# A gated delta-rule layer on one core: half the heads of the recurrence run one block and a boundary behind the other half, without constant products

## The reference

```
q, k, v = silu(conv(x Wq)), silu(conv(x Wk)) * 128**-0.5, silu(conv(x Wv))
a = sigmoid(x Wa + ba); beta = sigmoid(x Wb + bb)
for each token t, for each batch and head:       # state St is 128 x 128
    err = St k_t - v_t
    St  = a_t[:, None] * St - (beta_t * err)[:, None] * k_t[None, :]
    o_t = St q_t
o = layernorm(o) * sigmoid(x Wg) @ Wo;  x = layernorm(x + o)
x = layernorm(x + (silu(x Wu') * (x Wg')) @ Wd')     # ternary weights
```

## Time and profile before

| | us |
|---|---|
| median of 3 runs | 3010.08 (3008.52 to 3022.21) |
| the profiled execution, its own time | 3009.76 |
| its span, first to last instruction | 3008.0 |
| recurrence, first transposes of chunk 0 to those of chunk 15 | 1193.5 |
| the last chunk | 63.0 |

### The profile page before, as it was taken

One profiled execution on the slowest core, in us unless ns is written; L12 is line 12 of the kernel. 1 busy time (PEld: TensorE's weight loads), 2 busy tenths in 40 slices (PEclk: granted clock), 3 DMA queues, 4 the chain that ended last, 5 costly groups with the idle time before them and its releaser, 6 DMA issues. The chain is left out here.

```text
span 3008.0 us, 57441 instructions
## 1 busy us (share of the span) xinstructions
PE 2714.6 (90%) x18366; PEld 2291.7 (76%) x18366; DVE 2046.7 (68%) x5887; ACT 1191.7 (40%) x2377; POOL 1441.0 (48%) x1214
## 2 busy tenths in 40 slices
PE   8999999999995888988898988989865898699999
PEld 6888888888885777777787777877754777588887
DVE  5767868767783777777767777677746887533333
ACT  4454454454542222222222222222257876433333
POOL 3545345355365877677767777677622231000000
PEclk9999999999997999899989999899967999899999
DMA  5564664665557544344434444444455552400000
GB/s 123 143 198 134 164 178 136 171 177 141 172 149 250 199 184 184 138 172 175 160 137 184 183 184 178 159 183 183 172 214 196 208 191 106 168 8 10 14 10 14
DMA packets 417363, 454.86 MB, mean 151 GB/s; under 512 B 122496, under 2 KB 367232, under 8 KB 393856
## 3 DMA queue, kind: packets, MB, share of 16 engines
q1 hardware_dynamic: 417152, 452.22, 44.8%
HBM read 321.49 MB, written 131.14 MB: 150 GB/s over the span
## 5 line engine op out<-in xcount | busy, mean ns | idle before, releaser
L355 PE MATMUL pa_ps<-pa_x_hi,pa_w_hi 128*128 128x512 f32 x1296 | 507.5, 392 | 9.6 <-ACT pa_y L298 5.4
L355 PE MATMUL pa_ps<-pa_x_lo,pa_w_hi 128*128 128x512 f32 x1296 | 504.9, 390 | 0.0
L355 PE MATMUL pa_ps<-pa_x_hi,pa_w_lo 128*128 128x512 f32 x1296 | 504.9, 390 | 0.0
L438 DVE SCALAR_TENSOR_TENSOR pa_cv<-pa_y,pa_taps,pa_cv 128x2048 f32<-128x2048 f32 x144 | 355.9, 2472 | 17.8
L748 POOL TENSOR_TENSOR pb_gb<-pb_gb,pb_ng 128x448 f32<-128x448 f32 (+6 forms) x448 | 330.8, 783 | 57.8 <-DMA pb_ng<-scratch_ng 55.9
L1069 DVE TENSOR_TENSOR pb_tmp<-pb_gb,pb_ps 128x112 f32<-128x112 f32 (+6 forms) x1792 | 328.2, 220 | 19.4 <-POOL pb_gb L748 8.1
L1074 DVE TENSOR_TENSOR pb_ps<-pb_ps,pb_tmp 128x112 f32<-128x112 f32 (+6 forms) x1792 | 331.3, 226 | 6.3 <-DVE pb_tmp L1069 3.2
L943 PEld LDWEIGHTS pb_ps<-pb_Gm,pb_XT 128*128 128x128 f32 x2048 | 253.0, 199 | 68.9 <-issue 39.2
L355 PEld LDWEIGHTS pa_ps<-pa_x_hi,pa_w_hi 128*128 128x128 f32 x1296 | 243.6, 188 | 68.0 <-ACT pa_y L298 10.3
L732 POOL TENSOR_TENSOR pb_UT<-pb_UT,pb_crow 128x1024 f32<-128x1024 f32 x120 | 281.8, 2359 | 21.0 <-DMA pb_crow<-scratch_crow 20.3
L355 PEld LDWEIGHTS pa_ps<-pa_x_hi,pa_w_lo 128*128 128x128 f32 x1296 | 243.6, 188 | 51.2
(11 more groups left out here) (191 smaller groups left out, 5453.1 us busy)
## 6 DMA issues: line engine op xcount, KB each, us to landing
pb_crow<-scratch_crow SPq DMA_DIRECT2D x30, 2048.0 KB, 9.6
pb_gb<-scratch_pairs SPq DMA_DIRECT2D x64, 896.0 KB, 8.4
pa_o_ng<-scratch_beta SPq DMA_DIRECT2D x16, 1024.0 KB, 7.9
scratch_ng<-pa_o_ng SPq DMA_DIRECT2D x16, 1024.0 KB, 4.5
...
```

Source lines behind the costliest of these rows:

```text
L355: last = nc.tensor.matmul(out, w[:, mat, k, :], xx[:, k, b * S:(b + 1) * S], start=(k == 0 and n == 0), stop=(k == KT - 1 and n == 2))
L438: nc.vector.scalar_tensor_tensor(out=out, in0=yy[:, :, k:k + S], scalar=tap(k), in1=out, op0=ALU.mult, op1=ALU.add).then_inc(s_tap, 1)
```

## The change

In the recurrence the chunk becomes a cycle. Half 1 now runs one block and a chunk's boundary behind half 0: a cycle takes half 0 through blocks 0 to 3 of chunk c and half 1 from block 3 of chunk c-1 (with its state updates 2 and 3 and its starts of chunk c) to block 2 of chunk c. There is a first cycle, 14 middle ones and a last one, and behind it half 1's last block alone. Each engine's list and SP's is written out anew in this order, the ring places are new numbers, `T_PAST`/`D_PAST` step over places that a first or last cycle leaves out, and many semaphores are split by half. FILL is all zero and every other `busy` call of the cycles is gone, so no constant product is issued. `key_products` becomes `key_product`, one of the two tiles at a time. A new buffer `ngx` holds half 1's gates of blocks 2 and 3 (one ACT copy a cycle), so that `ng` can be reloaded before half 1 has done. The gates of block 0 are multiplied in on POOL at the end of the cycle before. Work per chunk is otherwise the same.

In the core of the diff below the lines that are left out are mostly removed ones.

```diff
...
+        ngx = m.sb("ngx", [P, HALF, CH // 2])
...
-        T_XT, T_XT_LAST = [0, 5, 10, 14, 18, 22, 28, 30], [0, 4, 8, 10, 12, 14, 16, 18]
-        t_xt = lambda n, hf, more: (T_XT if more else T_XT_LAST)[2 * n + hf]
-        t_later = lambda hf, more: 2 + (5 if more else 4) * hf
-        t_first = lambda hf: 16 + 8 * hf
-
-
-        D_START, D_CH = 10, 32
-        d_cross = lambda n, hf, more: 26 + hf if n == NBL - 1 and more else 2 * n + hf
-        D_STATE = [6, 10, 16, 22]
-        D_S = [14, 15, 20, 21, 28, 29, 30, 31]
-        D_S_FIRST = [22, 23, 24, 25, 28, 29, 30, 31]
-
-        FILL = [0, 0, 0, 0, 2, 0, 2, 4]
+        T_X = [[0, 9, 12, 20], [15, 25, 27, 5]]
+        T_LATER = [[2, 3], [14, 17]]
+        T_FIRST = [[24, 29], [30, 31]]
+        T_GRAM = [4, 7, 8, 11]
+        T_KT = [18, 19, 22, 23]
+        T_PAST = [{4: 3}, {}, {3: 2, 6: 3, 10: 2, 17: 3, 21: 4, 28: 9}]
+
+
+        D_START, D_CH = 6, 32
+        D_CROSS = [[0, 9, 15, 30], [16, 25, 31, 14]]
+        D_STATE = [17, 21, 1, 5]
+        D_S = [26, 27, 28, 29, 10, 11, 12, 13]
+        D_PAST = [{0: 9, 13: 2}, {}, {16: 9, 25: 5, 31: 15}]
+
+        FIRST, MIDDLE, LAST = range(3)
+        FILL = [0, 0, 0, 0, 0, 0, 0, 0]
...
+        solved = lambda c, n: 2 * (NBL * c + n + 2)
+        turn = lambda c, n, hf: 2 * NBL * c + [[0, 2, 3, 5], [4, 6, 7, 9]][hf][n] - 1
+        scaled = lambda c, n, hf: 27 * turn(c, n, hf) + 1
...
+            def cycle(c, p, kind, more2):
+                at, at_d = T_START + T_CH * c, D_START + D_CH * c
+                if kind != FIRST:
+                    sp.wait_ge(s_x[1], solved(c - 1, 3))
+                    load_gb(c, 3)
+                if kind == MIDDLE:
+                    sp.wait_ge(s_tp, at + T_X[1][3] + 1)
+                    load_rr(c + 1, 1 - p)
+                if kind == LAST:
+                    feed_forward_weights()
+                    store_o(c - 1, 1 - p, at_d)
+                    return
+                for j in range(4):
+                    write_gram(c + 1, at + T_GRAM[j], j)
+                compact(c + 1)
+                sp.wait_ge(s_us, 8 * c + 4)
+                load_crow(c, 1)
+                if kind != FIRST:
+                    store_o(c - 1, 1 - p, at_d)
+                sp.wait_ge(s_wv, 2 * c + 2)
+                sp.wait_ge(s_w, 2 * c + 2)
+                load(vt[:, :, :], "vt", c + 1, s_vl)
+                sp.wait_ge(s_gc, 16 * (BL - 1) * (c + 2))
+                sp.wait_ge(s_x[1], solved(c, 0))
+                load_gb(c + 1, 0)
+                sp.wait_ge(s_m, NBL * (c + 1))
+                sp.wait_ge(s_ngx, c + 1)
+                sp.wait_ge(s_sv, scaled(c, 3, 0))
+                sp.wait_ge(s_sv, scaled(c, 1, 1))
+                load(ng[:, :, :], "ng", c + 1, s_ngl)
+                sp.wait_ge(s_x[1], solved(c, 1))
+                load_gb(c + 1, 1)
                 if more2:
                     sp.wait_ge(s_tp, at + T_KT[3] + 1)
-                    sp.wait_ge(s_wn, 6 * c + 6)
-                    sp.wait_ge(s_rs, 6 * c + 6)
                     load_kq(c + 2, p)
                     sp.wait_ge(s_us, 8 * (c + 1))
                     load_crow(c + 1, 0)
-                if more:
-                    sp.wait_ge(s_x, solved(c, 3))
-                    load_gb(c + 1, 3)
-                sp.wait_ge(s_de, D_START + D_CH * c + d_cross(NBL - 1, 1, more) + 1 + 4)
-                sp.dma_start(flat(scr["o"][c, :, :, :]), flat(O[p][:, :, :])).then_inc(s_os[p], 16)
+                sp.wait_ge(s_x[1], solved(c, 2))
+                load_gb(c + 1, 2)
...
+            def cycle(c, lower, upper, p, kind):
+                at, at_d = T_START + T_CH * c, D_START + D_CH * c
+                more = kind != LAST
+
+                def rescale(n, hf):
+
+                    pool.wait_ge(s_tp, at + T_X[hf][n] + 2)
+                    xx = X[:, HALF * hf:HALF * (hf + 1), 0:BL * (n + 1)]
+                    by = rr[p][:, 0, HALF * hf:HALF * (hf + 1), n + 1:n + 2].broadcast_to([P, HALF, BL * (n + 1)])
+                    tt(xx, xx, by, ALU.mult).then_inc(s_rs[hf], 1)
+
+                less_v(c, at_d - D_CH + D_S[3], 0)
                 with_gates(c, 1)
+                pool.wait_ge(s_rl[p], 32 * lower + 32)
+                rescale(0, 0)
                 if more:
                     pool.wait_ge(s_crl, 32 * c + 16)
+                    pool.wait_ge(s_dp, at_d - D_CH + D_S[3] + 1)
                     decay(0)
+                masked(at + T_LATER[0][1], 1, 0)
+                if more:
                     decay(1)
                 with_gates(c, 2)
+                rescale(1, 0)
                 if more:
+                    decay(2)
+                    decay(3)
+                with_gates(c, 3)
+                rescale(2, 0)
+                less_v(c, at_d + D_S[7], 1)
+                rescale(0, 1)
+                masked(at + T_LATER[1][1], 1, 1)
+                if more:
+                    pool.wait_ge(s_crl, 32 * c + 32)
+                    pool.wait_ge(s_dp, at_d + D_S[7] + 1)
+                    decay(4)
+                    decay(5)
+                    decay(6)
+                rescale(1, 1)
+                if more:
+                    decay(7)
+                    with_gates(c + 1, 0)
+                rescale(2, 1)
+                if more:
+                    masked(at + T_FIRST[0][1], 0, 0)
+                    masked(at + T_FIRST[1][1], 0, 1)
...
+                copy_x(at, past, c, 0, 0)
+                key(T_LATER, 1, 0, 0)
+                key(T_LATER, 1, 0, 1)
+                next_gram(0)
+                absolutes(0)
+                if kind != FIRST:
+                    copy_x(at, past, c - 1, 3, 1)
+                next_gram(1)
+                next_gram(2)
+                absolutes(1)
+                copy_x(at, past, c, 1, 0)
+                next_gram(3)
+                absolutes(2)
+                act.wait_ge(s_ngl, 16 * (c + 1))
+                if kind != FIRST:
+                    act.wait_ge(s_sv, scaled(c - 1, 3, 1))
+                nc.scalar.activation(ngx[:, :, :], ng[:, HALF:HB, CH // 2:CH], ACT.Copy).then_inc(s_ngx, 1)
+                copy_x(at, past, c, 2, 0)
+                key(T_LATER, 1, 1, 0)
+                absolutes(3)
+                copy_x(at, past, c, 0, 1)
+                key(T_LATER, 1, 1, 1)
+                if more:
+                    copy_kt(0)
+                    copy_kt(1)
+                absolutes(4)
+                copy_x(at, past, c, 3, 0)
+                if more:
+                    copy_kt(2)
+                    copy_kt(3)
+                    key(T_FIRST, 0, 0, 0)
+                absolutes(5)
+                copy_x(at, past, c, 1, 1)
+                absolutes(6)
+                copy_x(at, past, c, 2, 1)
+                absolutes(7)
+                if more:
+                    key(T_FIRST, 0, 0, 1)
+                    key(T_FIRST, 0, 1, 0)
+                    key(T_FIRST, 0, 1, 1)
 
...
+                def products(first, pk):
+
+                    for r in range(2):
+                        pe.wait_ge(s_de, at_d + D_STATE[first // 2 + r] + 4 + 4)
+                        for j in (first + 2 * r, first + 2 * r + 1):
+                            state_products(at_d, D_S[j], pk, j, past_d.get(D_S[j], 1), fill=0)
+
+                x_transposes(at, past, c, 0, 0)
+                key(T_LATER, p, 1, 0, 0)
+                cross(at, at_d, past_d, c, 0, 0)
+                key(T_LATER, p, 1, 0, 1)
                 if more:
+                    pe.wait_ge(s_kq[1 - p], 32 * upper + 32)
+                next_gram(0)
+                if kind != FIRST:
+                    x_transposes(at, past, c - 1, 3, 1)
+                next_gram(1)
+                if kind != FIRST:
+                    state(at, at_d, 2)
+                next_gram(2)
+                x_transposes(at, past, c, 1, 0)
+                if kind != FIRST:
+                    state(at, at_d, 3)
+                cross(at, at_d, past_d, c, 1, 0)
+                next_gram(3)
+                if kind != FIRST:
+                    products(4, p)
+                else:
                     for j in range(4, 8):
+                        state_products(at_d, D_S[j], p, j, past_d.get(D_S[j], 1))
+                x_transposes(at, past, c, 2, 0)
+                if kind != FIRST:
+                    cross(at, at_d, past_d, c - 1, 3, 1)
+                cross(at, at_d, past_d, c, 2, 0)
+                key(T_LATER, p, 1, 1, 0)
+                x_transposes(at, past, c, 0, 1)
+                key(T_LATER, p, 1, 1, 1)
+                cross(at, at_d, past_d, c, 0, 1)
+                key_transposes(0)
+                key_transposes(1)
+                x_transposes(at, past, c, 3, 0)
+                key_transposes(2)
+                key_transposes(3)
+                if more:
+                    state(at, at_d, 0)
+                    key(T_FIRST, 1 - p, 0, 0, 0)
+                x_transposes(at, past, c, 1, 1)
+                if more:
```

(54 more changed lines are left out.)

442 lines of the change are left out of this document (167 added, 275 removed).

## The result

| | before | after |
|---|---|---|
| median, us | 3009.3 (3006.6 to 3022.2) | 2932.5 (2921.7 to 2938.9) |
| profiled execution, us (span) | 3009.76 (3008.0) | 2936.22 (2934.5) |
| mean granted clock of the span | 0.960 | 0.933 |

The ratio is 0.973, 95% interval 0.969 to 0.978: faster by 2.7%, where 5.1% (2856 us) was forecast. The direction was right, the gain was half of what the sum gave.

A forecast was written before the change was run, and what follows sets the result against it. Bound by a chain through DVE, ACT and PE plus clock falls; DVE's floor 60.4 us. Periods of 68.5 for 79.6 us save 166, ends cost 12: 154 less, 2856 us; own range 2830 to 2890, eight in ten 2761 to 3025.

The forecast's parts named there:

- The walk of a middle cycle: Middle cycle in the new order: walked to 66.4 us; with clock and loop terms, 68.5 us.
- Which wait ends last: Block 1: POOL's late gates hold DVE's solve 2.7 us; PE's transposes start at 19.4 us instead of 16.5.
- Rival 1: Gates in time, no PE gap, clock holds, DVE's work alone counts: period 62.2 us, 2761 us; chance 0.12.
- The clock in every cycle: Fall each cycle behind PE's 3.2 us gap before block 1's transposes, adding 1.2 to 1.5 us.
- My own signs of being wrong: POOL's order doesn't delay the solve, clock falls elsewhere, or last cycle takes over 25 us more.
- What brings it back: Behind PE's gap: eight transposes and a state block, 5 us without a gap, bring the clock back.
- Rival 3: Only a long run of key products brings the clock back: period 99 us, 3313 us; chance 0.17.
- Rival 2: Clock returns late; PE at 1.2 GHz through cross and state products: period 77.6 us, 2992 us; chance 0.23.
- The state block at 1.2 GHz: PE's state block at the lower clock, shown in no row: 2.1 us, or 3.5 to 4; 3.5 taken.
- The loop: Periods with PE's late start are 1.6 to 2 us longer, about one in two: 0.9 us a period.
- Constants: Of 46 removed a chunk, 20 in PE's gapless stretch gain 4.3 us; 26 lie in waits, save nothing.
- The ends: Old half 1 some 10 us late, half 1 alone about 11, first cycle 11 shorter: +12 us, bounds 0 and 25.

The follow-up runs named there:

- run 10: Changed kernel with cycles written out, block 1's gates a cycle earlier, and ACT's copy of half 1's last block before the first gram's copy: 2854.5 us, ratio 0.949.
- Run 3: Changed kernel with POOL's gates of block 1 multiplied in one cycle earlier: 2910.2 us, ratio 0.967.
- run 6: Changed kernel with the loop over the cycles written out on every engine: 2907.1 us, ratio 0.966.
- Run 2: Changed kernel with the 46 constant products a cycle put back at the same operations: 2982.4 us, ratio 0.988.
- run 1: Kernel before, in the old order, with only its constant products left out: 3216.6 us, ratio 1.066.
- runs 12: run 10 plus earlier weight loads, spread sums, and constant products in the last cycle, tail and first cycle's transposes: 2825.8 us, ratio 0.938.
- run 4: Changed kernel without the 48 absolute sums of the feed-forward weights and the weights' loads for them: 2913.7 us, ratio 0.963.

## Why the prediction was off, point by point

*The walk of a middle cycle: right in sum, in part by luck.* An undisturbed period is 68.1 us; the walk gave 66.4 and 1.2 for the clock. The waits for cross and state products went, POOL's gates came: 2.57 and 1.35 us where I had 2.7 and, for block 2, about nothing. But two errors cancelled. The cross update of block 1 came at 24.5 us (1711.98 less 1687.51), not at 26.5, since the clock did not fall ahead of it; from the last start of half 1 to the end it took 33.8 us where I had 30.6, with 2.17 us of wait for a state block and a fall of the clock that the walk has not. The floor of 60.4 us was not reached: in run 10 DVE is busy 59.0 us of a period of 65.1.

*Which wait ends last: half right.* I had the gates release PE's transposes and named nothing behind them. Run 3 shows the state blocks 1 to 2.5 us behind; the gates were worth 1.8 us, not 3.9. Rival 1 would have had the period at 62.2; with the gates in time it is 66.3. Part of what was missing was ACT's order: the copy of half 1's last solution sits behind a gram's copy, so its transposes start 13.0 us into the cycle (1700.50, the solve at 1687.51). PE then had this work where the walk had it idle, and the gap ahead of block 1's transposes was 1.1 us long instead of 3.2. With the copy moved (run 10) the first state block is in time and 1.0 us comes back; the wait of 2.4 us ahead of the second stays, and what ends it was not tried.

*The clock in every cycle: wrong place, and the sum larger.* I had a fall behind PE's gap ahead of block 1, 19 us into the cycle. None is there. Every undisturbed period has one of 3.4 or 6.8 us, 37 to 41 us into the period; two of the six with a jump have none, four have one of 6.8 or 13.7 behind the jump, and three others one of 13.7 at 42 to 44. The sum of low clock in the middle is 109 us, 7.8 a period, where I had 3 to 7. That the price of a short fall (1.2 us) came near is chance, since it was worked out for other work: in run 6 periods with a fall are 0.9 to 2.3 us longer than those without. My own signs of being wrong named a fall elsewhere, and a last cycle over 25 us longer; both came.

*What brings it back: right as far as seen.* At 1779.0 it rose in a run of transposes, 32-column grams and a state block, without a constant product. Rival 3, worked out for a kernel that needs a long run of key products, would have given 3313 us and didn't occur; the rule in "TensorE: Matmul & The Clock Gate", Part 4, of the Trainium skill, by which transposes don't engage the full clock, did not decide here, and since the grams stand in the same run, no run isolates the transposes. Rival 2's sight, PE without a gap and still at 1.2 GHz, did occur: not in the middle, but for 25.5 us in the last stretch, which has a cross product, state products, transposes and short cross products.

*The state block at 1.2 GHz.* 3.1 us long, 3.0 to the next start, between the two prices I gave (2.1, and 3.5 to 4); I took 3.5.

*The loop: mis-sized.* I took the 0.9 us a period of before, from periods that are 1.6 to 2 us longer, and named only PE's stall. DVE stalled there as well, 2.6 to 2.8 us at six jumps (`DVE pb_ps L1041 <- issue`). In the new order DVE's stall, 2.7 to 3.0 us, stands ahead of the first solve. By itself it costs much the same as before: periods 9 and 13, which have it and no fall, are 1.7 to 2.5 us longer than run 6's periods without a fall. What I had at nothing, beyond the 1.2 us of clock in every cycle, is what it sets off. Before, short falls of 3.4 us stood behind two of the six jumps; now falls of 6.8 or 13.7 stand behind four, and the three of 13.7 in periods 1, 8 and 12 are gone too with the loop written out. Together it is 2.7 us a period by run 6.

*Constants: right that they cost time here and gave clock there.* I had 20 of 46 on the old path, 4.3 us. Run 2 gives 5.0 us a period, but in the new order and less the clock that they brought, so that the two numbers are close is no proof of the 4.3. That constants gave clock shows in the old order, where leaving all 46 out cost 14.9 us a period (run 1). The new order needs them no longer in the middle; I take the reason to be that it fills PE's waits with work of the other half, which no run isolates.

*The ends: the step that failed.* I took +12 us on top of fifteen equal gains of 11.1, with bounds of 0 and 25. For the first cycle that is 22 us less (11.1 and the 11 of old work that half 1 lacks); it took 2.4 more. The work is missing, as I said: DVE is busy 48.5 us for 59.3. But its waits grew by 13 us. These are DVE's waits in the first cycle, before and then after:

```profile
DVE pb_tmp L1069 <- POOL pb_gb L748: 8.1, 1, 8.1
DVE pb_ps L1060 <- DMA pb_ng<-scratch_ng: 6.3, 1, 6.3
DVE pb_ps L1090 <- POOL pb_W L739: 5.9, 1, 5.9
DVE pb_ps L1084 <- PE pb_ps L943: 4.2, 4, 1.3
```

```profile
DVE pb_ps L1181 <- PE pb_ps L1004: 16.9, 4, 6.5
DVE pb_tmp L1168 <- POOL pb_gb L767: 11.3, 2, 9.2
DVE pb_ps L1159 <- DMA pb_ng<-scratch_ng: 7.6, 1, 7.6
```

Half 0 is alone there, so each cross product is waited for (16.9 us for 4.2), and the clock is low for 55 us instead of 17. What the clock alone takes can be read across the runs in the new order. Their first cycles, whose lists differ a little, line up by it: 83.2 and 84.4 us with 17 us of low clock (runs 12 and 2, with constants), 84.8 with 31 (run 10), 88.9 with 41 (run 4), 93.9 with 55 (the changed kernel), 96.9 with 61 (run 6). So some 10 of the 24.5 us that the forecast missed there are clock; the other 14 are waits that stay at the old low clock: the 11 us were work on DVE, and not on the path, where the chain of half 0 is. At the end it is the same with half 1: I had 23 us (the terms I named, 10 and 11, make 21), it is 41.7, of them 15 the clock, 10.7 work that was in the chunk before, 16 waits in the chain of one half. I charged the clock in the middle, where the other half keeps PE fed, and not at the ends, where nothing does.

*How the miss adds up.* Forecast 154 us, measured 73.5 between the two profiled executions, so 80.5 are missing: the middle 34 (14 x 11.1 = 155 for 121.2), the first cycle 24.5, the last stretch 18.7, the later stages 4.5 (the diff doesn't touch them, and I leave their cause open), less 0.8 ahead of the recurrence: 81. Of the middle's 34, 25 are the loop's (14 x 1.8) and 4 the old period, which is 79.3 by this mile-post where the forecast had 79.6.
